# One slot less between the q product and the attention stages of a software-pipelined transformer block

## What is computed

```
xn  = layernorm(x)
qkv = xn @ Wqkv.T + bqkv
q, k, v = heads of qkv      # for each of the 2048 columns b: 8 rows n attend to 8 rows m
scores = mask + 32**-0.5 * einsum('bnd,bmd->bnm', q, k)
attn = softmax(scores);  out = einsum('bnm,bmd->bnd', attn, v)
x + (out @ Wproj.T + bproj) + (fp8(xn) @ fp8(Wffn).T + bffn)
```

## Time and profile before

| | |
|---|---|
| median of 3 runs | 1569.23 us (1569.12 to 1570.31) |
| profiled execution | 1569.3 us, span of its instructions 1567.5 us |
| mean granted clock of the tensor engine | 0.982 of full speed |
| busy: PE, DVE, POOL, ACT | 96%, 92%, 88%, 67% of the span |
| slots | 143 (0 to 142) |

### The profile page before, as it was taken

One profiled execution on the slowest core, in us unless ns is written; L12 is line 12 of the kernel. 1 busy time (PEld: TensorE's weight loads), 2 busy tenths in 40 slices (PEclk: granted clock), 3 DMA queues, 4 the chain that ended last, 5 costly groups with the idle time before them and its releaser, 6 DMA issues. The chain is left out here.

```text
span 1567.5 us, 23119 instructions
## 1 busy us (share of the span) xinstructions
PE 1506.4 (96%) x6913; PEld 681.0 (43%) x6913; DVE 1442.0 (92%) x1188; ACT 1048.3 (67%) x2010; POOL 1378.9 (88%) x1046
## 2 busy tenths in 40 slices
PE   4999999999999999999999999999999999999956
PEld 3444444444444444444444444444444444444412
DVE  7389999999999999999999999999999999999992
ACT  5676667676766767666776776676776667776432
POOL 1288999899899989999998999999899999999885
PEclk8999999999999999999999999999999999999977
DMA  5334454545455454544545455454544445454322
GB/s 197 76 89 113 113 124 118 128 113 128 118 121 121 116 132 106 132 116 125 123 109 134 111 127 122 119 124 111 134 112 128 119 116 128 113 131 97 91 78 81
DMA packets 366508, 184.00 MB, mean 117 GB/s; under 512 B 314160, under 2 KB 314160, under 8 KB 366384
## 3 DMA queue, kind: packets, MB, share of 16 engines
q1 hardware_dynamic: 366384, 182.53, 47.5%
HBM read 73.41 MB, written 33.55 MB: 68 GB/s over the span
## 5 line engine op out<-in xcount | busy, mean ns | idle before, releaser
L391 POOL TENSOR_TENSOR prod_pv<-kv,probs 128x2048 f32<-128x2048 f32 x192 | 699.3, 3642 | 10.0
L758 DVE TENSOR_REDUCE o_nat<-prod_pv 128x512 f32<-128x2048 f32 (+1 forms) x128 | 429.1, 3352 | 51.7 <-POOL prod_pv L391 34.9
L725 DVE TENSOR_REDUCE scores<-prod_qk 128x64 f32<-128x2048 f32 x192 | 439.3, 2288 | 6.6
L720 DVE TENSOR_TENSOR prod_qk<-q_ps,kv 128x1536 f32<-128x1536 f32 (+1 forms) x192 | 397.8, 2072 | 2.2 <-ACT kv L557 2.2
L602 PE MATMUL proj_ps<-wproj_hi,oT 128*128 128x512 f16 x1032 | 339.2, 390 | 0.0
L602 PE MATMUL k_ps<-wqkv_hi,xT 128*128 128x512 f16 x1024 | 327.0, 381 | 5.4 <-DMA xT<-x 5.1
L602 PE MATMUL v_ps<-wqkv_hi,xT 128*128 128x512 f16 x1024 | 325.4, 379 | 0.0
L602 PE MATMUL q_ps<-wqkv_hi,xT 128*128 128x512 f16 x1024 | 325.4, 379 | 0.0
L566 ACT ACTIVATE kv<-v_ps 128x512 f32<-128x512 f32 x128 | 142.3, 1112 | 156.3 <-PE v_ps L602 156.2
L602 PE MATMUL proj_ps<-wproj_lo,oT 128*128 128x512 f16 x516 | 202.1, 392 | 0.0
L602 PE MATMUL k_ps<-wqkv_lo,xT 128*128 128x512 f16 x512 | 195.1, 381 | 0.0
(11 more groups left out here) (117 smaller groups left out, 1853.4 us busy)
## 6 DMA issues: line engine op xcount, KB each, us to landing
xn<-in_L_attn_x SPq DMA_DIRECT2D x128, 256.0 KB, 2.8
xs<-in_L_attn_x SPq DMA_DIRECT2D x128, 256.0 KB, 2.6
out<-xs SPq DMA_DIRECT2D x128, 256.0 KB, 2.1
xT<-x SPq DMA_TRANSPOSE x256, 3.0
kv<-in_L_attn_Wqkv SPq DMA_DIRECT2D x3, 1024.0 KB, 10.4
oT<-o SPq DMA_TRANSPOSE x128, 3.2
kv<-in_L_ffn_weight SPq DMA_DIRECT2D x1, 1024.0 KB, 5.6
kv<-in_L_attn_Wproj SPq DMA_DIRECT2D x1, 1024.0 KB, 14.3
```

What stands on the lines that cost most here:

```text
L391: nc.gpsimd.tensor_tensor(o, v, p, ALU.mult).then_inc(pv_multiplied, 1)
L720: nc.vector.tensor_tensor(prod_qk[:, 1:1 + m0 + 4 - m1, :], qb, k, ALU.mult).then_inc(qk_multiplied, 1)
L725: nc.vector.tensor_reduce(scores[:, n % 2, :, m0:m0 + 4].rearrange("p h m -> p m h"), prod_qk[:, row:row + 4, :].rearrange("p m (h d) -> p ...
L758: nc.vector.tensor_reduce(o_nat[:, n % 2, :], prod_pv[:, place:place + units, :].rearrange("p q (c m) -> p c q m", m=4), AX_XY, ALU.add).t ...
```

## The change

The lags of all stages from the first key's product to the projection become one less: 6 to 14 in place of 7 to 15. The lags of statistics, centring, normalising, k/v and q (1 to 5) stay. No instruction, buffer or wait is added or taken away. The waits count tiles, so each still waits for the same piece of work; only how many slots lie between a piece of work and its use is changed. The program has 142 slots in place of 143.

```
-L_STATS, L_CENTRE, L_NORM, L_KV, L_Q, L_FIRST, L_QK, L_SHIFT, L_SOFT, L_PV, L_SUM, L_RES, L_SPLIT, L_LIN, L_PROJ = \
-    1, 2, 3, 4, 5, 7, 8, 9, 10, 11, 12, 12, 13, 14, 15
+    1, 2, 3, 4, 5, 6, 7, 8, 9, 10, 11, 11, 12, 13, 14
```

## The result

| | before | after |
|---|---|---|
| median of 19 runs, us | 1569.38 (1568.35 to 1570.63) | 1572.65 (1570.53 to 1574.16) |
| span of the profiled execution, us | 1567.5 | 1570.0 |
| ratio of the times | | 1.0018, 95% interval 1.0011 to 1.0025 |

The new lags cost 3.3 us, 0.2%, in the median, and the interval of the ratio lies above 1. The forecast was 1569.3, the range 1565.5 to 1574.0.

A forecast was written before the change was run, and what follows sets the result against it. The prediction took a relay of DVE and POOL, not the tensor engine, as the bound. Its terms, +2.85 for k, -3.3 in the head and +0.5 in the tail, sum to +0.05: 1569.3 us, range 1565.5 to 1574.0.

The forecast's parts named there:

- the head gains nothing: Rival: DVE's heavy stretch at the start begins at 103.46 as before, so 1572.65 us; chance 0.08.
- The relay: Middle: DVE works about 68.8 us, hands to POOL for about 22.9, POOL hands back; 91.78 us a group.
- The slackened wait: ACT's 83.7 us of waits for DVE before refilling q_ps go away; worth nothing.
- q for the first key: ACT's q copy now waits for q of the slot just done, 1.5 us later in role 75; steady cost 0.
- The race for k: Each group, DVE's second product of tile 4 waits 0.19 us for k of tile 7; 15 groups, +2.85 us.
- The head: At the start, tile 4's second product begins at 100.2 instead of 103.46, limited by tile 7's k: -3.3 us.
- The tail's rstd: Near the end, POOL's role 130 now contains the last rstd, 550 ns: +0.5 us.
- The last group: Role 132, last of the fifteen groups: DVE's wait for k counted at 0.19 us like the others.
- the third rival: k of tile 7 comes much later; a further 0.5 us a group gives 1576.8 us; chance 0.17.
- Distance 92.0: Sign in the profile after: DVE's waits for POOL lie 91.9 to 92.0 us apart.
- The last k product: Sign at the end: the forecast is wrong if it starts much less than 93 us before the end.
- The tensor engine's weight loads: Sign: the tensor engine waits more for its transposed input xT, about 0.45 us a group.

The follow-up runs named there:

- experiment 4: The kernel before with only the first of the four fp8 linear matmuls of each tile: 1569.13 us, ratio 0.9997.
- Experiments 1 to 3: New lags, k copied ahead of the linear copies: 1569.78 us; five tiny ACT copies ahead of the k copy, new lags: 1578.62, old lags: 1569.41.
- experiment 8: The changed kernel with only the first of the four fp8 linear matmuls of each tile: 1569.77 us, ratio 1.0004 to the kernel before.

## Why the prediction was right, and where its numbers were off

The measured median lies in the range, 3.3 us above the forecast, and part of that is luck. The mechanisms that I named are there, but the forecast said no change, and the runs show a small loss, at the edge of the 0.2% that I had called slower (3.3 us, ratio 1.0018). The upper end of the range was there for a k that comes much later in every group; what filled it were one group at the end and gaps that no step had. That the median equals the 1572.65 of the rival "the head gains nothing" is chance: the head did gain.

- **What bounds the kernel: right.** The relay, not the tensor engine: 48 us less of the tensor engine's busy time left the time within the noise (experiment 4, 0.9997, 0.9988 to 1.0007), and DVE and POOL kept 91.8.
- **The slackened wait and q for the first key: right.** ACT's wait for DVE is gone and worth nothing; its waits for q come to 64.2 us, and the k copy still starts 9.62 us after DVE's reduction.
- **The race for k: mechanism right, size low.** 0.25 us a group, forecast 0.19. The late start is 0.15 (from copy to product 0.66 us, not the 0.70 I took from the head), and from the product that has waited to its reduction it is 0.06 longer, which the sum had left out; 0.03 stand in DVE's wait for POOL, without a cause. Experiments 1 to 3 show cause and price.
- **The head: right.** Forecast -3.3, found -3.2 for the late start of that execution corrected (-2.7 without).
- **The tail's rstd: right**, +0.5.
- **The last group: mis-sized.** I gave it 0.19 like the others; it took 0.98, because the tensor engine's input is late there and there is no slack left. With less work for the tensor engine it is gone (experiment 8: 4.44 us from first to second product instead of 5.37). It is the third rival at a single place.
- **What no step had:** the four gaps in DVE's program, 1.3 us, and the late k behind the transpose of 1014.07, 0.3 us in two groups. Before the change 12 us between k copy and product hid any late input; the sum kept a single number for every group.
- **Also not foreseen:** 1.3 us given back in the last slots, at a higher granted clock. What changed the clock was not tried, and not every execution with the new lags has it. The times of after's 19 executions go with the clock of the whole execution: the 8 with a mean granted clock of 0.984 or more have a median of 1571.3 us, the 11 with 0.983 or less one of 1572.9. The profiled one, at 0.986, belongs to the first.
- **Signs.** Distance 92.0: as said. The last k product is 91.2 us before the end of the span (1478.85 of 1570.0), where I had said 93: again the last group, and the last slots' speed. The tensor engine's weight loads waited 10.6 us more for their input, about 0.7 us a group, where I had said 0.45.

The profiled execution of after took 1571.87, 2.6 us more than the forecast. The terms are 14 x 0.06 + 0.8 = 1.6 for the race for k, 1.3 for the gaps, 0.3 for the late k of two groups, 0.1 for the head, 0.5 for the late start, less 1.3 in the last slots: 2.5. The median lies another 0.8 above this execution, which has one of the higher clocks; that the clock is the cause is not shown.

## What to carry to other kernels

Pulling a consumer closer to its producer in a pipeline gains once, at the fill, and costs in every round in which the edge has no slack left; count that slack in the profile (here 837.64 - 837.13 = 0.51 us between two starts that need 0.66) before taking the slot out. When two engines hand work to and fro, look for the handover and not for the fullest engine, and before reordering one of them, count what the new order costs on that engine itself. Change the order only in the slots where the other one waits: that brought 8.9 us where the same change in all slots left the length of a group as it was and lost 4.4, 3.95 of them in the head.

## What was not expected of the hardware

- DVE stops 0.25 to 0.37 us at places fixed in its program, apart by multiples of about 68 instructions, when a short instruction stands before them; where the instruction behind such a place waits for another engine, it starts 0.35 us later than usual even behind a reduction of 2.29 us.
- SP takes 1.8 to 2.6 us instead of 1.23 to issue an xT transpose, 7 or 8 times in 256, before the change as after it.
- DVE's row maximum behind the reduction that it reads starts 2.32 us after that one's start, a second product behind a reduction after 2.42, another instruction after 2.20; over a whole group such neighbours cost about 1.5 us.
- DVE's second product takes 2.29 us when it has waited for k and 2.23 in the same place without that wait, and the reduction behind it starts 0.06 us later.
